# A selected-LSTM kernel on TensorE: the repeat of a wrong guess inside the leaf, and the projection with its chunks outermost

## What is computed

```python
logits = concatenate([h, c, x_t]) @ W_sel.T + b_sel
s      = argmax(logits)                       # of S = 4 sets
g      = W_ih[s] @ x_t + W_hh[s] @ h + b_ih[s] + b_hh[s]   # 4 x 512 gates
c      = sigmoid(f) * c + sigmoid(i) * tanh(g_)
h      = sigmoid(o) * tanh(c)
```

## Time and profile before

| | |
|---|---|
| median of 3 runs | 6864.05 us |
| the profiled execution's own time | 6865.91 us |
| its span | 6864.20 us |
| PE busy | 6126.8 us, 89% |
| PE weight loads (PEld) | 4106.7 us, 60% |
| DVE busy | 3617.9 us, 53% |
| ACT, POOL busy | 1804.5 us, 1685.8 us |
| mean granted TensorE clock | 0.955 |
| chain that ended last, largest shares | PE L1007 33%, PE L1069 15%, PE L1016 8%, issue 6% |

### The profile page before, as it was taken

The page is one execution under the profiler, slowest core; times in us unless marked ns, Lnnn a source line. Parts: engine busy times, 40 slices in busy tenths (PEclk is TensorE's granted clock), DMA queues, the critical chain, the costliest instruction groups (busy, mean ns, idle before and its releaser), DMA issues.

```text
span 6864.2 us, 340774 instructions
## 1 busy us (share of the span) xinstructions
PE 6126.8 (89%) x126674; PEld 4106.7 (60%) x126675; DVE 3617.9 (53%) x19152; ACT 1804.5 (26%) x6561; POOL 1685.8 (25%) x4128
## 2 busy tenths in 40 slices
PE   6727999679999999999999999999999999999986
PEld 3423444566666666666666666666666666666664
DVE  5453111235555556555665555566556665565555
ACT  1001000412233233222332332233333333233321
POOL 5732111412222222222222222222222222222220
PEclk8758999579999999999999999999999999999999
DMA  3220000522222122222222222222222222222210
GB/s 94 1 77 0 0 0 0 177 70 60 60 61 61 57 61 62 58 60 61 64 63 61 62 61 61 60 62 64 61 61 63 64 63 61 60 63 61 61 52 27
DMA packets 715589, 389.97 MB, mean 57 GB/s; under 512 B 47835, under 2 KB 703579, under 8 KB 715296
## 3 DMA queue, kind: packets, MB, share of 16 engines
q1 hardware_dynamic: 684322, 369.66, 18.4%
q0 software_dynamic: 24192, 0.10, 1.1%
q10 hardware_dynamic: 7038, 19.69, 0.9%
HBM read 370.96 MB, written 18.38 MB: 57 GB/s over the span
## 4 chain that ended last, share of the span: by engine, by line
PE 70%; issue 6%; DVE 6%; DMA 0%; DVEq 0%; SPq 0%; POOL 0%; ACT 0%; POOLq 0%
PE ps L1007 33%; PE ps L1069 15%; PE ps L1016 8%; PE ps L1000 5%; PE ps L996 4%; DVE hsum L837 2%; PE ps L993 2%; PE ps L983 2%; DVE osum L845 1%; DVE acts L855 1%; DVE gates L842 1%; DVE osum L848 1%; DVE cprod L851 0%; PE ps L972 0%; DMA wring<-in_w_ih 0%
## 5 line engine op out<-in xcount | busy, mean ns | idle before, releaser
L1007 PE MATMUL ps<-WH,hparts 128*2 128x384 f16 x49760 | 2297.3, 326 | 194.4 <-issue 173.2
L837 DVE TRANSPOSE_TENSOR_REDUCE hsum<-ps 128x12 f32<-128x384 f32 x1250 | 728.8, 583 | 1784.5 <-PE ps L1007 1774.2
L1007 PEld LDWEIGHTS ps<-WH,hparts 128*2 128x2 f16 x49760 | 1042.4, 83 | 1046.7 <-issue 297.0
L1069 PE MATMUL ps<-xcur,wcur 128*128 128x64 f32 x9728 | 1342.8, 281 | 89.1 <-issue 15.1
L1069 PEld LDWEIGHTS ps<-xcur,wcur 128*128 128x128 f32 x9728 | 1179.3, 191 | 276.6 <-issue 213.6
L449 POOL COPY xT<-hfull 128x4 f32 x1250 | 239.5, 192 | 3721.7 <-DVE hfull L866 3721.7
L465 POOL COPY wcur<-wring 128x512 f32<-128x512 f32 x1216 | 743.4, 611 | 449.7 <-ACT gxb L593 447.8
L1016 PEld LDWEIGHTS ps<-WH,hparts 128*2 128x2 f16 x40000 | 596.7, 83 | 359.0 <-issue 316.6
L1016 PE MATMUL ps<-WH,hparts 128*2 128x128 f16 x40000 | 775.4, 219 | 8.6
L578 ACT ACTIVATE gx_now<-gxb 128x16 f32 x1250 | 269.7, 216 | 1832.6 <-DVE pick L831 1709.3
L963 PE MATMUL ps<-O,Adj 128*128 128x512 f16 x3000 | 650.3, 380 | 77.2 <-DVEq L743 77.2
(11 more groups left out here) (147 smaller groups left out, 5001.8 us busy)
## 6 DMA issues: line engine op xcount, KB each, us to landing
wring<-in_w_ih SPq DMA_DIRECT2D x1280, 256.0 KB, 2.9
gxb<-in_w_hh ACTq DMA_DIRECT2D x32, 512.0 KB, 4.0
adjacency<-Adj SPq DMA_DIRECT2D x2, 6400.5 KB, 24.7
Adj<-adjacency SPq DMA_DIRECT2D x10, 640.0 KB, 7.3
sim<-adjacency SPq DMA_DIRECT2D x10, 640.0 KB, 6.5
adjacency<-total,where_ POOLq DMA_INDIRECT x168
x_rows<-X SPq DMA_DIRECT2D x1, 2560.0 KB, 8.7
wring<-x_rows SPq DMA_DIRECT2D x10, 256.0 KB, 3.6
```

The lines of the kernel that those rows point to most:

```text
L837: dve.tensor_reduce(hsum[:, :], gate_ps.rearrange("p (c q) -> p c q", q=32), AX.X, ALU.add, apply_transpose=True).then_inc(turned, 1)
L1007: last = nc.tensor.matmul(gate_ps[32 * j:32 * j + 2, :], hparts[:, k, :], WH[:, s * KC + k, part, j, 0:3 * P], start=(k == 0 and part == 0 ...
L1069: last = nc.tensor.matmul(unit_ps, wcur[:, k, :], xcur[:, k, :], start=(k == 0), stop=(k == KC - 1))
```

## The change

Three edits. In the projection the chunk k becomes the outer loop and the unit u the inner one: each slot of the ring now holds one chunk of all four units of a gate, the four units accumulate side by side in their four banks, three of four slots are freed by the last product that reads them, and TensorE waits for its own products once in a group of four units. The wait for owsel moves one product ahead. A wrong guess's gate products are repeated in the leaf itself, in the Else branch of the comparison, which holds three copies, one for each other set; the tree behind it then holds only the output gate's products.

```diff
-                    for u in range(SUB):
-                        sp.wait_ge(wring_free, sp.snap(q * (G * SUB) + (g * SUB + u + 1)))
-                        load_unit(q, g, u)
+                    for k in range(KC):
+                        sp.wait_ge(wring_free, sp.snap(q * (G * KC) + (g * KC + k + 1)))
+                        sp.dma_start(wring[:, k, :, :].rearrange("p u n -> p (u n)"),
+                                     w_ih[:, bass.ds(q, 1), order[g], k * D:(k + 1) * D].rearrange("p a n -> p (a n)")
+                                     ).then_inc(wring_in[k], 16)
...
             with pe.Fori(0, SG) as q:
-                for u in range(SUB):
-                    pe.wait_ge(wring_in[u], pe.snap(q * 16 + 16))
-                    pe.sem_inc(pieces_seen, 1)
-                    pe.wait_ge(proj_out, pe.snap(q * SUB + (u + 1)))
-                    for k in range(KC):
-                        last = nc.tensor.matmul(ps[:, 4 + u, 0:TB], wring[:, u, k, :], xT[:, k, 0:TB], start=(k == 0), stop=(k == KC - 1))
-                    last.then_inc(proj_mm, 1)
-                    pe.wait_ge(proj_mm, pe.snap(q * SUB + (u + 1)))
-                    pe.sem_inc(wring_free, 1)
+                for k in range(KC):
+                    for u in range(SUB):
+                        if u == 0:
+                            pe.wait_ge(wring_in[k], pe.snap(q * 16 + 16))
+                            pe.sem_inc(pieces_seen, 1)
+                        if k == 0:
+                            pe.wait_ge(proj_out, pe.snap(q * SUB + (u + 1)))
+                        last = nc.tensor.matmul(ps[:, 4 + u, 0:TB], wring[:, k, u, :], xT[:, k, 0:TB], start=(k == 0), stop=(k == KC - 1))
+                        if k == KC - 1:
+                            last.then_inc(proj_mm, 1)
+                        elif u == SUB - 1:
+                            last.then_inc(wring_free, 1)
+                pe.wait_ge(proj_mm, pe.snap(q * SUB + SUB))
+                pe.sem_inc(wring_free, 1)
...
                 for k in range(SUB):
+                    if k == SUB - 1:
+                        pe.wait_ge(owsel_ready, n)
                     nc.tensor.matmul(logit_ps, acts[:, 3 * SUB + k:3 * SUB + k + 1], wselT[:, k, :], start=False, stop=False)
                 pe.wait_ge(tanc_ready, n)
-                pe.wait_ge(owsel_ready, n)
...
                     with pe.If_eq(chosen, S - s):
                         pe.sem_inc(settled, 1)
                         output_products(s)
-
-                def repeated(s):
-                    cell_products(s, settled)
-                    output_products(s)
+                    with pe.Else():
+                        one, two, three = [other for other in range(S - 1, -1, -1) if other != s]
+                        with pe.If_lt(chosen, S - two):
+                            cell_products(one, settled)
+                        with pe.Else():
+                            with pe.If_lt(chosen, S - three):
+                                cell_products(two, settled)
+                            with pe.Else():
+                                cell_products(three, settled)
 
                 of_set(guess, guessed)
                 with pe.If_ne(chosen, guess):
-                    of_set(chosen, repeated)
+                    of_set(chosen, output_products)
```

## The result

The changed kernel takes **10521.11 us** (median of 4 runs, 10491.08 to 10539.73), against 6866.62 us for the kernel before beside it (6862.68 to 6872.74): 1.532 times as long, 95% interval 1.527 to 1.536. The forecast was 6802 us; what came is the second rival, the loop that no longer stays loaded.

The account below looks back on a forecast made before the run. Bound: one chain per step of TensorE's gate products, DVE and ACT, wrong guesses costing 2.06 us more. Terms 36 + 50 + 3 - 5 - 22 = 62 us off 6865.9 gave 6803.9 profiled, 6802 us beside the median; eight-in-ten range 6745 to 6880.

Parts of the forecast that it names:

- second rival: Step loop: the longer code no longer stays loaded, 4.2 us a reload, 7830 us at one step in five; chance 0.20.
- part 6: TensorE's loop code: 1.4 times as much, five more loading stalls of 4.4, 22 us lost; once loaded, it stays.
- Part 1: Wrong guesses: fewer branches before the repeat save 0.165 us in each of 305, 50 us; bounds 24 to 76.
- part 2: Tree moved behind the repeat: output products may slip, 5 us lost; bounds 0 and 30.
- part 3: Right guesses: the leaf of set 0 gets a jump over its new Else; cost 0, bound 7 us.
- Part 5: Projection: fewer drains and an earlier first transfer, 36 us gained, bounds 21 and 41; groups take 8.2 us.
- first rival: Projection: TensorE's clock rises to 2.4 GHz there, 42 us more saved, 6760 us; chance 0.13.
- fourth part: Logits: waiting for owsel a product earlier gains 3 us; bounds -10 and +15.

Follow-up runs that it names:

- e3: Changed kernel with 201 never executed instructions ahead of its first step loop and 41 ahead of the second: 6782.24 us, 0.9885 of the kernel before.
- e12: Kernel before with 129 unexecuted instructions in each of the four leaves and 201 more ahead of the first loop: 7097.11 us.
- e6: Kernel with the projection's edit and later owsel wait alone, plus 5 never executed instructions ahead of the first loop: 6830.16 us, 0.9954 of the kernel before.
- e7: Kernel before with 249 never executed instructions ahead of the first step loop: 6932.37 us, 1.0104 of the kernel before.
- e4: Changed kernel with the wrong guesses' repeats back behind the tree, keeping the projection's edit and later owsel wait: 6910.65 us, 1.0078 of the kernel before.
- e2: Kernel before with 449 unexecuted instructions behind a branch in the wrong guesses' path, in both step loops: 7080.29 us.
- e5: Kernel before with 129 unexecuted instructions in each of the four leaves, behind the output products: 15739.31 us.

## Why the prediction was wrong

**The step that failed is part 6**, "once loaded, the loop stays", and the "seven blocks of eight" by which the rival was given 0.20. Rows 9 showed only that a loop of 1234 instructions stays. I divided the changed loop's length, 1765 by the prediction's count, by 256 and did not ask where the loop begins. At its offset of 66 it runs through eight blocks and asks for nine. The text had both terms, one block more for a loop that isn't aligned and one ahead; together they decided against the forecast, and I gave them a chance in place of adding them. In place of a loop that stays the run showed 1550 fetches in 1194 steps and 3598 us more than the same loop takes in e3, where it needs eight blocks and has no fetch. The sizes of that rival were off as well: 1.3 fetches a step, not one in five or one, at 2.3 us and not 4.2. Of these 3598 us, TensorE's busy time explains about 970 (5764.86 us for 116676 products, against 4726.57 for 114975 from 1500 to 6500 of e3, scaled by the counts); the other 2630 it stood still, 1.7 us a fetch.

The Trainium skill ("Runtime: NRT & Kernel Launch", Instruction fetch mechanics) has 2048 instructions in blocks of 256 for TensorE, eight blocks, which agrees with eight that stay and nine that don't. It also says that a long kernel need not fit and that crossing a block's end is mostly hidden. For a loop the measurements decide against both: a loop that doesn't fit pays 2.2 to 2.4 us a fetch, and in one that does, an end inside the unit products still adds 0.05 to 0.07 us on average.

**Part 1 was right, mechanism and size.** In e3 TensorE's loads wait for issue before a repeat for
```profile
PEld ps L1015 <- issue: 218.2, 291, 1.1
```
0.750 us on average, where the earlier trace rows give 0.956 and I expected 0.79. One wrong step of e3, with a guess of set 2 and set 3 chosen:
```profile
3165.11 3.03 PE L1015 MATMUL ps<-WH,hparts 128*2 128x384 f16 x64
...
3165.51 0.15 DVE L833 TENSOR_REDUCE pick<-lmark 1x1 int32<-1x4 f32 x1
...
3166.66 1.08 PEld L1015 LDWEIGHTS ps<-WH,hparts 128*2 128x2 f16 x32 [0.48 <-issue]
3167.81 0.59 PEld L1024 LDWEIGHTS ps<-WH,hparts 128*2 128x2 f16 x32
...
3170.51 0.75 PEld L1015 LDWEIGHTS ps<-WH,hparts 128*2 128x2 f16 x24 [0.18 <-DVE hparts L871]
```
From the end of pick to the repeat are 1.00 us, 1.41 before; the step takes 5.40 us and the products of both sets form one row of 64 without a pause. By the three ways through the leaf's tests, the wrong steps take 5.457, 5.758 and 5.852 us, before 5.828, 5.847 and 5.939: 0.37, 0.09 and 0.09 less. Summed over their 288 (94, 99 and 95) that is 52 us; the first way, one test not taken, gives two thirds of it.

**Parts 2 to 4.** L1024's loads start 1.15 us behind the repeat's, just as L1016's did, and the step is not late: part 2 cost nothing that the 52 us don't contain. Right steps went from 3.783 to 3.790 us (6 us), nearly all in the leaf of set 0, 3.793 to 3.825, as in e12 (3.816), which has that jump over an Else too: part 3's bound of 7. The wait for owsel lost 0 to 6 us instead of gaining 3: within its bounds, wrong in sign.

**Part 5 was right.** The timeline of the projection in the changed kernel:
```profile
1268.85 1.97 PE L987 MATMUL ps<-xT,wring 128*128 128x64 f32 x8 [17.41 <-DMA wring<-in_w_ih]
...
1278.58 7.08 PE L987 MATMUL ps<-xT,wring 128*128 128x64 f32 x32 [1.07 <-DVE gxb L801]
1286.58 7.09 PE L987 MATMUL ps<-xT,wring 128*128 128x64 f32 x32 [0.91 <-DVE gxb L801]
...
1390.54 7.08 PE L987 MATMUL ps<-xT,wring 128*128 128x64 f32 x32 [0.90 <-DVE gxb L801]
```
A group takes 8.00 us (8.2 expected, 10.13 before), the first starts 5.2 us earlier than in the earlier trace rows (5 expected), and the clock stays at 0.50, so the first rival is out. (Its price was too small for its own rows: four times 1.97 less 1.10 is 3.5 us a group, not 2.8.) e6 has 36.5 us at the first h, where 36 were forecast. So close a match is partly luck: with the same projection the first h comes 30 to 39 us earlier in the other kernels, largely by how long TensorE waits for issue at the loop's entry.

**With the loop loaded, the sum holds.** e3 stands 79 us below the kernel before (6785.3 and 6864.2 of span): 30 to the first h, 13 in the first 20 steps, 45 in the first loop, 10 lost in the second; forecast were 62, or 84 without the 22 for loading. That the sum comes within 5 us of those 84 is in part luck, since e3's padding moved some of it. At the entry of the first loop e3 waits 16.63 us for issue ahead of L1000, where the kernel before waits 6.88 ahead of L993. And some 8 of the 13 us in the first 20 steps come with padding ahead of the loop alone: e7, which has nothing else of e3, takes 98.0 us there with 1 fetch, for 105.6 with 6. So four of the terms (parts 1, 2, 3 and 5) were sound, the fourth part had its sign wrong at little cost, and a premise under all of them was false: the sum priced each instruction that is executed and took for granted that each is there.

## What to carry to other kernels

Before code is added to an engine's loop, count its compiled instructions and where it starts: take the blocks that it executes and the one behind each, and if these are more than stay loaded (eight here), the reloads outweigh any saving of the size sought here (1.3% gained against 53% lost). When a time moves by a per cent after an edit far from the loop, compare the gaps between single instructions before explaining it by the edit: a block's end may have moved. An unexecuted pad ahead of the loop tests both in one run, and can be the remedy.

## What the runs showed that I had not expected

- A block's end in straight code costs 0.05 to 0.07 us a step, on average, at the unit products though nothing is fetched, and five instructions of padding ahead of the loop were worth 80 us of 6910 (e4 to e6), more than either part of the change.
- Sections of code that are jumped over count when they follow an executed block: the padding of e2 was harmless in one copy of the loop and cost 133 us in the other, where it lies otherwise to the blocks' ends.
- Reloads lower the granted clock: a mean of 0.76 in the loop with 1.3 fetches a step and 0.65 from 1500 to 6500 in e5 with 3.0, against 1.00; a right step that is partly at 0.50, without any fetch, takes 5.73 us instead of 3.80.
- A loop that overflows by one block is not reloaded in full each round: the changed kernel fetches 1.3 blocks a step, and 605 of 1195 steps see none.
